# Expert weights in three transfers, laid out by halves of the inner units

## The reference

```python
def body(acc, inp):
    g, u, d, we = inp
    y = jax.nn.silu(x @ g.T) * (x @ u.T) @ d.T
    return (acc + we[:, None] * y, None)
out, _ = jax.lax.scan(body, jnp.zeros_like(x), (gate_proj, up_proj, down_proj, cw.T))
...
return (out + shared).reshape(B, S, H)
```

## Time and profile before

| what | value |
|---|---|
| median of 3 runs | 1507.28 us (1506.95 to 1507.31) |
| the profiled execution's own time | 1501.42 us |
| its span | 1499.7 us |
| TensorE busy in the span | 1261.5 us (84%) |
| VectorE busy | 1353.0 us (90%) |
| ScalarE busy | 971.4 us (65%) |
| GpSimd busy | 784.2 us (52%) |
| the 47 tiles | 786 to 1325 us from the span's start |

### The profile page before, as it was taken

How to read it: one execution, slowest core, us unless ns; L and a number is a source line. 1 busy time by engine, 2 the same in 40 slices (tenths; PEclk the granted TensorE clock), 3 DMA queues, 4 the chain that set the end, 5 groups by cost and what they waited for, 6 DMA issues and landing times. The chain is left out here.

```text
span 1499.7 us, 14543 instructions
## 1 busy us (share of the span) xinstructions
PE 1261.5 (84%) x4518; PEld 721.7 (48%) x4518; DVE 1353.0 (90%) x1319; ACT 971.4 (65%) x1528; POOL 784.2 (52%) x411
## 2 busy tenths in 40 slices
PE   7785796899699868996989998899988899826998
PEld 3331242443244324442556666566666666615555
DVE  4999999998999899988898988999899999888894
ACT  5766568575864666625866788767887767734442
POOL 0465566545555553550465555555565665565632
PEclk9799999999999998998899999999999999977999
DMA  7444545535544443450356678677777887755531
GB/s 254 109 141 127 126 141 142 154 98 151 133 146 124 127 127 109 126 154 2 99 181 233 239 260 291 230 272 239 254 275 230 286 273 273 270 183 147 167 100 57
DMA packets 99837, 264.31 MB, mean 176 GB/s; under 512 B 10832, under 2 KB 11344, under 8 KB 93616
## 3 DMA queue, kind: packets, MB, share of 16 engines
q1 hardware_dynamic: 87936, 225.36, 48.4%
q0 software_dynamic: 11440, 37.50, 7.7%
q10 hardware_dynamic: 384, 0.52, 0.1%
HBM read 233.73 MB, written 29.62 MB: 176 GB/s over the span
## 5 line engine op out<-in xcount | busy, mean ns | idle before, releaser
L457 POOL TENSOR_TENSOR state<-state,bc_rows 128x1024 f32<-128x1024 f32 x254 | 599.2, 2359 | 613.6 <-DVE banks L1702 613.5
L1095 PE MATMUL banks<-state,ident 128*128 128x512 f32 x640 | 323.7, 638 | 106.6 <-POOL state L457 106.6
L1710 DVE TENSOR_TENSOR_SCAN state<-decay,banks 128x1024 f32<-128x1024 f32 x176 | 402.0, 2284 | 11.4 <-DVE banks L1702 5.0
L1702 DVE TENSOR_TENSOR banks<-du,bc_rows 128x1024 f32<-128x1024 f32 x256 | 314.5, 1229 | 13.4 <-DVE state L1710 0.5
L1185 PE MATMUL banks<-z_gate,expert_w 128*128 128x256 f32 (+1 forms) x1504 | 284.1, 347 | 7.5 <-DMA expert_w<-in_moe_w 7.5
L1185 PEld LDWEIGHTS banks<-z_gate,expert_w 128*128 128x128 f32 x1504 | 248.8, 191 | 60.1 <-issue 18.9
L1095 PEld LDWEIGHTS banks<-state,ident 128*128 128x128 f32 x640 | 118.0, 197 | 282.0 <-POOL state L457 170.0
L712 ACT ACTIVATE decay<-delta,neg_a 128x511 f32<-128x511 f32 x352 | 226.4, 710 | 16.8 <-DVE state L1710 11.6
L1710 DVE TENSOR_TENSOR_SCAN state<-expert_w,banks 128x1024 f32<-128x1024 f32 x80 | 182.9, 2286 | 6.9 <-ACT expert_w L712 4.2
L1196 PE MATMUL banks<-expert_w,hidden 128*128 128x512 f32 x316 | 156.2, 610 | 2.3 <-ACT expert_out L776 1.2
L1721 DVE TENSOR_TENSOR y_scan<-y_scan,state 128x1024 f32<-128x1024 f32 x94 | 114.3, 1216 | 3.6 <-POOL state L457 2.0
(11 more groups left out here) (318 smaller groups left out, 1659.2 us busy)
## 6 DMA issues: line engine op xcount, KB each, us to landing
bc_rows<-bc_d SPq DMA_DIRECT2D x208, 512.0 KB
expert_w<-in_moe_w SPq DMA_DIRECT2D x48, 1536.0 KB, 9.1
ys_d<-expert_out SPq DMA_DIRECT2D x32, 512.0 KB, 5.4
ctx_t<-in_ctxT SPq DMA_DIRECT2D x8, 512.0 KB, 6.7
x_res<-in_x SPq DMA_DIRECT2D x4, 1024.0 KB, 10.7
xn_d<-y_scan SPq DMA_DIRECT2D x4, 1024.0 KB, 7.7
ys_d<-expert_out SPq DMA_DIRECT2D x15, 256.0 KB, 5.9
out_x<-x_res SPq DMA_DIRECT2D x3, 1024.0 KB, 6.0
```

The lines of the kernel that those rows point to most:

```text
L457: nc.gpsimd.tensor_tensor(W[:, c % 4], W[:, c % 4], bcast2(BC[:, u, 1, :]), ALU.mult).then_inc(mulc_done, 1)
L1095: mm = nc.tensor.matmul(PS[:, m], ID[:, :], W[:, c % 4, m, :], start=False, stop=True, skip_group_check=True)
L1702: nc.vector.tensor_tensor(drive(s), DU[:, s % 2, 2 * h:2 * h + 2, :], bcast2(BC[:, u, 0, :]), ALU.mult).then_inc(mulb_done, 1)
L1710: nc.vector.tensor_tensor_scan(flat(W[:, c % 4]), flat(DAS[c % da_slots(s, i)]), flat(drive(s)), 0.0, ALU.mult, ALU.add).then_inc(scan_don ...
```

## The change

The weights of a tile come in three transfers of 512 KB: part 0 holds gate and up for the first half of the inner units, part 1 for the second half, part 2 the down projection. The packed array is laid out anew for it, so that each part is one stretch of 4 KB in a partition. Each part has its own semaphore in each slot. Parts 0 and 1 of tile j wait only for the matmuls of tile j - 2 that read that part (`gu_done`), part 2 waits for `y_done` as before. The register load moves ahead of these waits. TensorE waits for a part where it first reads it. The shared expert's weights, still one transfer, follow the new layout.

```diff
-            def load_tile_w(j, slot):
-                if j >= 2:
-                    sp.wait_ge(y_done, DONE[j - 1])
+            def load_tile_w(j, parts):
+
                 at = expert_at(j)
                 e = sp.value_load(TE[0:1, at:at + 1], min_val=0, max_val=NE - 1)
-                sp.dma_start(MW[:, slot, :], t["moe_w"][bass.ds(e, 1), :, :].rearrange("a p n -> p (a n)")
-                             ).then_inc(tw_in[slot], 16)
+                for part in parts:
+                    if j >= 2 and part < IT:
+                        sp.wait_ge(gu_done, (j - 2) * 2 + part + 1)
+                    elif j >= 2:
+                        sp.wait_ge(y_done, DONE[j - 1])
+                    lo = part * WGU
+                    sp.dma_start(MW[:, j % 2, lo:lo + WGU], t["moe_w"][bass.ds(e, 1), :, lo:lo + WGU].rearrange(
+                        "a p n -> p (a n)")).then_inc(tw_in[j % 2][part], 16)
...
             def tile_in(j):
                 u, n = j, P * BLOCKS[j]
-                pe.wait_ge(tw_in[u % 2], 16 * (j // 2 + 1))
                 pe.wait_ge(xst_ready, 2 * j + 2)
                 for it in range(IT):
+                    pe.wait_ge(tw_in[u % 2][it], 16 * (j // 2 + 1))
                     pe.wait_ge(h_ready, j * 2 + (it - 1 + PRE_H))
                     for g in range(2):
                         for k in range(ET):
-                            at = g * WGU + k * INNER + it * P
+                            at = it * WGU + (g * ET + k) * P
...
             def tile_out(j, it):
                 u = j
                 pe.wait_ge(h_ready, j * 2 + (it + 1 + PRE_H))
+                pe.wait_ge(tw_in[u % 2][IT], 16 * (j // 2 + 1))
...
-        rows = [w.transpose(0, 2, 1).reshape(n, ET, P, INNER).transpose(0, 2, 1, 3).reshape(n, P, WGU) for w in (gate, up)]
+        both = [w.transpose(0, 2, 1).reshape(n, ET, P, IT, P).transpose(0, 2, 3, 1, 4) for w in (gate, up)]
+        rows = [np.stack(both, axis=3).reshape(n, P, 2 * WGU)]
```

More of the change, by code:

```diff
@@ L178, in build @@
         xs_in = [sem(f"xs_in{i}") for i in range(2)]
-        tw_in = [sem(f"tw_in{i}") for i in range(2)]
+        tw_in = [[sem(f"tw_in{i}_{part}") for part in range(IT + 1)] for i in range(2)]
         ys_stored, out_stored = sem("ys_stored"), sem("out_stored")
@@ L383, in _ @@
                     sp.wait_ge(shdown_done, QT * NB)
-                    load_tile_w(0, 0)
+                    load_tile_w(0, range(IT + 1))
             def tile_turn(s, i):
@@ L401, in tile_turn @@
                     if m + 1 < NTILE:
-                        load_tile_w(m + 1, (m + 1) % 2)
+                        load_tile_w(m + 1, range(IT + 1))
                     if m:
@@ L416, in _ @@
             for i in range(2):
-                sp.wait_ge(tw_in[i], 16 * ((NTILE - i) // 2))
+                for part in range(IT + 1):
+                    sp.wait_ge(tw_in[i][part], 16 * ((NTILE - i + 1) // 2))
             sp.dma_start(BW, t["base_wT"].rearrange("(k p) n -> p k n", p=P)).then_inc(ld_ffn1, 16)
```

## The result

The changed kernel's median is 1499.26 us over 9 runs, against 1507.31 us of the kernel before over 9 runs; the ratio of the two is 0.993, with a 95% interval of 0.9908 to 0.9952. The forecast was 1500.1 us. Times of one kernel spread widely here: 1492.71 to 1501.79 us for the changed one, 1505.49 to 1513.75 us for the one before.

A forecast was written before the change was run, and what follows sets the result against it. VectorE and TensorE, both nearly full in the tiles, bound the kernel, with TensorE waiting for weights. Removing 6.0 us of waits in the last stage and 1.2 us earlier gives 1507.28 - 7.2 = 1500.1 us, range 1497 to 1505.5.

The forecast's parts named there:

- What bounds the tiles, and the seven waits: In the 47 tiles VectorE and TensorE are both nearly full; TensorE's matmuls wait 7.5 us for `expert_w`, all to vanish.
- 1.2 of 1.4 us: Weight waits in stages before the last: 1.4 us, of which 1.2 us was counted because VectorE has more to do there.
- tiles ending near 1318: Sign that the forecast is right: the tiles end near 1318 us on the profile's timeline.
- The whole wait is passed on through 0.4 us of room on VectorE: At tile 44 all 1.75 us gained reaches tile 45, since the second `hidden` is 0.4 us short of binding.
- Rival A: Another engine, VectorE or ScalarE, takes over the wait in the tiles; only 2.4 us gained, time 1504.9; 12%.
- Costs taken as nothing: Per tile, two more SyncE issues (0.8 us), three more TensorE waits and shorter rows were all counted as free.
- Rival B: Added TensorE waits between gate-and-up halves and ahead of down projection halves cost 42 ns each; time 1506.0, or slower; 7%.
- The start 1.2 us earlier: At tile 44 SyncE issues part 0 at about 1284.3 instead of 1285.51; it lands 4 to 5 us later.
- The fit that the prediction takes from the Trainium skill: Transfer time as 2.0 us plus bytes over 436 GB/s, putting a tile's first part there after 3.2 us.
- The sum: TensorE's weight waits give 6.0 us in the last stage and 1.2 us earlier, 7.2 us; bounds 0 and 7.5.
- Assuming that the gain carries over unchanged from the profiled execution to the median: The 7.2 us from the profiled 1501.42 us was subtracted from the median 1507.28 us, giving 1500.1 us.
- Rival C: More is gained: TensorE's 16.4 us weight-load waits are all real and earlier traffic eases gathers; time 1490.9; 5%.

The follow-up runs named there:

- the run with a third of the bytes: The kernel before, loading only the down projection's 512 KB per weight transfer from tile 2 on; stretch 526.4 us, ratio 0.9959 to the kernel before.

## Why the prediction came out as it did

- *What bounds the tiles, and the seven waits*: right. All are gone. Two of the seven lie behind a full tile, not one: 0.99 us at tile 39 and 0.30 us at tile 42. The wait of 0.35 us at tile 26 gave nothing back (from tile 25 to 31 it takes 70.2 us in both kernels), as the prediction allowed for with its 1.2 of 1.4 us. From tile 43 to 44 it takes 8.59 us, a little less than the 8.7 to 8.9 that were forecast. The sign "tiles ending near 1318" did not come: TensorE's last matmul of tile 46 ends at 1326.1 in the first profile, where tile 0 was late, and at 1320.5 and 1320.8 in the two others (1325.5 before).
- *The whole wait is passed on through 0.4 us of room on VectorE*: right in the last stage, the step called most open to error. In the first profiles of both kernels tile 44 gains 1.9 us for a wait of 1.75 us, tile 35 1.7 for 1.72, tile 38 1.3 for 1.27. Rival A is refuted with it.
- *Costs taken as nothing*: right. Met waits were tested alone, more issues and shorter rows together. An issue was not 0.36 us, though: with three in a row the last takes 1.0 us in the middle, and some take up to 1.8. Rival B is refuted.
- *The start 1.2 us earlier*: it did not come, and was not needed. In the middle of the tiles part 0 goes out 0.6 to 0.9 us after the start of the tile before, against 0.89 us for the whole transfer before. A part lands after 7.4 us, not 4 to 5, the first of a tile after 6.8. By the prediction's own times, 1284.3 and 1293.4, that leaves 1.7 us and not 4. In the changed kernel tile 44's first part went out at 1287.42, landed at 1294.78 and was needed at 1295.70: 0.9 us of room, and 0.4 us at tile 38. The fit that the prediction takes from the Trainium skill ("DMA: Bandwidth & Descriptors", the anatomy section) is for transfers issued by GpSimd, and these are SyncE's; its estimate of 3.2 us for the first part is half of what was measured.
- *The sum*: too small. This is the step that failed: "bounds 0 and 7.5 for what TensorE's row can give". It took the waits of one execution for the whole price. The four profiles of the kernel before give a mean stretch of 533.6 us, the three of the changed kernel 521.7 us, a gain of 11.9 us; the three timed comparisons give 8.1, 14.8 and 12.2 us between medians. The waits themselves were sized nearly right, 7.8 us in the mean of the four. Read off between the same tiles of both kernels, 11.9 us are made up of
  - 7.4 us of waits for weights (7.8 less the 0.4 us at tiles 26 and 27, which give nothing back);
  - 0.9 us because each of the other waits, 5.5 in the mean, costs 0.16 us more than its row says: a row's end is modelled, and without a wait the next matmul begins 0.16 us ahead of it (1306.44 against 1304.72 + 1.88);
  - 2.1 us of half-clock blocks behind such waits, five in four profiles at 1.7 us each;
  - 0.9 us of lower clock between tiles 16 and 17, see above. It falls there also in the run with a third of the bytes, which has no late weights, so late weights are not needed for it; its cause is open;
  - 0.6 us at tile 1. Ahead of it TensorE waits 1.2 to 2.1 us for gathered rows in each of the seven profiles in which tile 1's weights come in one transfer (row below), 1.2 us with two parts, and not at all in seven of the eight profiles with three or six parts (0.6 us in the eighth).

```profile
795.17 0.63 PE L1164 MATMUL banks<-ident,y_scan 128*128 128x128 f32 x4 [1.71 <-DMA y_scan<-xn_d,selected]
```

- *Assuming that the gain carries over unchanged from the profiled execution to the median*: wrong, and the same fault. The profile was 5.9 us faster than the median, which was seen and not asked about. That execution had none of the blocks that the change removes, and its tile 0 began 0.9 to 8.7 us earlier than in the other three.
- *Rival C* (more gained than the sum, 5%) ended nearest. Its weight-load row was not the reason; its easier gathers are, for the 0.6 us at tile 1. Most of the rest came from the clock, which no part of the prediction named.

## What to carry to other kernels

A wait of TensorE costs its own length and sometimes the clock after it; sum both, and look at the granted clock behind each wait, in several profiles. When the profiled execution stands well off the median of the runs, profile it again before a sum is made from it: here the sum of waits was steady within 0.9 us, the price of the stretch was not within 4 us. Split a late transfer by the order in which its parts are read, before trying to start it earlier; here the splitting gave the gain and the earlier release nothing that can be seen.

## What the hardware showed that was not expected

- In this traffic a smaller transfer lands little sooner as long as the rest of the tile's weights is under way beside it: 9.1 us for 1536 KB, 7.4 us for one of three of 512 KB, 5.8 us for one of six of 256 KB; 512 KB without the others took 5.7 us.
- Waits for weights of 1.98 to 2.95 us were followed by a block at half clock in 7 of 8 cases, those up to 1.82 us never. But behind the 2.39 us for `hidden` in tile 16 the clock fell in all four profiles of the kernel before and in none of the three of the changed one: the length of the one wait is not the whole condition.
- GpSimd's issue of an indirect transfer takes about 1.0 us or about 1.9 us, and which of the two differs between executions of one and the same kernel.
- A wait that is already met costs TensorE at most 4 ns between matmuls in flight (564 of them, at most 2 us).
